# ScalarE copies a batch's turned probabilities ahead of the next batch's exponentials

## The reference

```python
xn, ln = layernorm(ctx), layernorm(layernorm(x))      # 64 + 64 rows a batch
q = ln @ Wq + bq
k, v = split(concat([xn, ln]) @ Wkv + bkv)
sim = einsum('bhid,bhjd->bhij', q * 128**-0.5, k)      # 8 heads x 64 x 128
out = einsum('bhij,bhjd->bhid', softmax(sim), v)
x = x + tanh(g_xattn) * (merge_heads(out) @ Wo + bo)
probs = softmax(layernorm(x) @ Wr + br); top 2 of 8 experts
x = x + tanh(g_ffn) * sum_e weight_e * (relu(layernorm(x) @ W1_e + b1_e) @ W2_e + b2_e)
```

## Time and profile before

| what | value |
|---|---|
| median of 3 runs | 795.09 us (794.71 to 797.86) |
| profiled execution: time | 800.09 us |
| profiled execution: span, first to last instruction | 798.4 us |
| granted TensorE clock, mean | 0.991 |
| busy: PE | 761.3 us, 95% of the span |
| busy: ACT | 497.8 us, 62% |
| busy: DVE | 525.9 us, 66% |
| busy: POOL | 443.1 us, 55% |
| DMA | 119.42 MB, mean 150 GB/s |

### The profile page before, as it was taken

The page is one execution under the profiler, slowest core; times in us unless marked ns, Lnnn a source line. Parts: engine busy times, 40 slices in busy tenths (PEclk is TensorE's granted clock), DMA queues, the critical chain, the costliest instruction groups (busy, mean ns, idle before and its releaser), DMA issues.

```text
span 798.4 us, 17460 instructions
## 1 busy us (share of the span) xinstructions
PE 761.3 (95%) x5392; PEld 645.5 (81%) x5392; DVE 525.9 (66%) x1829; ACT 497.8 (62%) x1630; POOL 443.1 (55%) x455
## 2 busy tenths in 40 slices
PE   7999999999999999999999999999999999879788
PEld 7778777777888988788988788988878889768665
DVE  4636677685857567677658777767768556465536
ACT  3677767676866566766556576656568655445622
POOL 2233264646552444785656686565668465466663
PEclk9999999999999999999999999999999999999999
DMA  6745151542455542174654146575316456534523
GB/s 196 199 161 193 59 210 71 210 145 81 145 186 158 200 153 71 41 231 160 214 195 146 47 109 219 189 230 172 104 44 199 146 191 205 162 107 122 149 77 87
DMA packets 119791, 119.42 MB, mean 150 GB/s; under 512 B 14585, under 2 KB 94994, under 8 KB 119698
## 3 DMA queue, kind: packets, MB, share of 16 engines
q1 hardware_dynamic: 111088, 102.41, 39.0%
q0 software_dynamic: 7680, 15.74, 6.7%
q10 hardware_dynamic: 930, 0.15, 0.1%
HBM read 35.94 MB, written 41.55 MB: 97 GB/s over the span
## 4 chain that ended last, share of the span: by engine, by line
PE 79%; DVE 6%; issue 6%; ACT 4%; POOL 2%; another core or an unknown queue 2%; DMA 1%; SPq 1%; ACTq 0%; DVEq 0%; POOLq 0%
PE shared L1426 14%; PE batch L1364 12%; PE batch L1377 12%; PE hid_ps L1294 8%; PE xy_ps L1308 7%; PE batch L1372 6%; PE shared L1217 3%; PE shared L1219 3%; PE shared L1218 3%; PE batch L1308 2%; ACT probs L746 2%; PE xy_ps L1271 2%; PE batch L1354 1%; PE shared L1415 1%
## 5 line engine op out<-in xcount | busy, mean ns | idle before, releaser
L676 POOL TENSOR_TENSOR probs<-probs,rsums 128x512 f32<-128x512 f32 x128 | 132.9, 1038 | 234.3 <-DVE rsums L1147 232.0
L746 ACT ACTIVATE probs<-batch,neg_max 128x128 f32<-128x128 f32 x512 | 180.5, 374 | 2.0 <-DVE neg_max L1151 2.0
L651 POOL DMA_INDIRECT sorted_x<-xn,row_of x120 | 121.3, 1011 | 36.0 <-issue 28.0
L827 ACT ACTIVATE qT<-shared,tb 128x512 f32<-128x512 f32 x128 | 87.2, 696 | 85.4 <-PE shared L1219 75.8
L1377 PE MATMUL batch<-pT_sb,kvn 128*128 128x512 f32 x256 | 134.2, 606 | 5.5 <-ACT pT_sb L754 5.4
L1364 PE MATMUL batch<-kvT,qT 128*128 128x128 f32 x1024 | 135.4, 275 | 0.8 <-ACT qT L827 0.8
L1426 PE MATMUL shared<-M,oT 128*128 128x128 f32 x1024 | 125.3, 275 | 0.2
L1364 PEld LDWEIGHTS batch<-kvT,qT 128*128 128x128 f32 x1024 | 124.4, 192 | 1.2 <-ACT qT L827 1.2
L1426 PEld LDWEIGHTS shared<-M,oT 128*128 128x128 f32 x1024 | 119.5, 192 | 1.3 <-issue 1.3
L746 ACT ACTIVATION_READ_ACCUMULATOR probs<-batch,neg_max 128x1 f32 x512 | 110.3, 215 | 0.0
L761 ACT ACTIVATE oT<-batch 128x512 f32<-128x512 f32 x128 | 76.2, 595 | 47.6 <-PE batch L1377 42.6
(11 more groups left out here) (168 smaller groups left out, 1241.7 us busy)
## 6 DMA issues: line engine op xcount, KB each, us to landing
wt<-wall SPq DMA_DIRECT2D x124, 321.0 KB
sorted_x<-yg SPq DMA_DIRECT2D x36, 512.0 KB, 4.9
xt<-sorted_x SPq DMA_DIRECT2D x162, 64.0 KB
sorted_y<-y_sb SPq DMA_DIRECT2D x78, 128.0 KB
kv<-in_ctx_dram SPq DMA_DIRECT2D x16, 256.0 KB
kv<-in_x_dram SPq DMA_DIRECT2D x16, 256.0 KB
xres<-in_x_dram SPq DMA_DIRECT2D x32, 128.0 KB
out_dram<-x SPq DMA_DIRECT2D x15, 256.0 KB
```

The lines of the kernel that those rows point to most:

```text
L651: nc.gpsimd.indirect_dma_start(xs[k % SETS][:, :], bass.IndirectOffsetOnAxis(ap=row_of[:, g, choice, c:c + 1], axis=0), xn[:, g % 2, c, :] ...
L676: nc.gpsimd.tensor_tensor(pv, pv, rsums[:, m % 2, :].unsqueeze(2).broadcast_to([P, 4, P]), ALU.mult).then_inc(probs_ready, 1)
L746: last = nc.scalar.activation(probs[:, m % 2, c * P:(c + 1) * P], batch_ps[m % BANKS][:, c * P:(c + 1) * P], ACT.Exp, bias=neg_max[:, m % ...
L827: nc.scalar.activation(qT[:, g % 2, :, number, :], sh[:, :].rearrange("p (b i) -> p b i", b=GB), ACT.Identity, bias=tb[:, number:number + ...
```

## The change

ACT's `slot(n)` copies the turned probabilities of batch n - 2 before the exponentials of batch n - 1. The operations, their waits and their numbers stay the same; only their order on ACT's list differs. The instructions of the other engines are the same.

```diff
             def slot(n):
                 if 0 <= n - OUT - 1 < B:
                     keep_product(n - OUT - 1)
+                if 0 <= n - TURN < B:
+                    keep_turned(n - TURN)
                 if 0 <= n - EXP < B:
                     exponentials(n - EXP)
-                if 0 <= n - TURN < B:
-                    keep_turned(n - TURN)
                 g = n // GB - 1
                 if n % GB == 6 and 0 <= g < G:
                     act.wait_ge(route_step, ROUTE * g + 2)
```

## The result

The changed kernel took 817.38 us (median of 4 runs, 816.08 to 819.68) against 796.47 us of the kernel before (median of 4, 794.71 to 797.86): a ratio of 1.0265, 95% interval 1.0241 to 1.0290, which is 19.2 to 23.1 us slower. The forecast was 817.0. The two totals agree better than the differences do: the forecast added 21.9 us to a median of 795.09, and the measured difference is 20.9 from a median that now stands 1.4 us higher. The profiled execution took 819.68 us, 19.59 more than that of before. Its page says where: PE is busy about as long as before (761.3 us there), in a span that is 19.6 us longer.

The account below looks back on a forecast made before the run. PE was taken to set the time throughout. Slots without tiles through POOL +10.7, queries behind DVE +11.2, tile slots and product 0: +21.9 us on the median 795.09 gives 817.0, range 803 to 829 (chance 0.80).

Parts of the forecast that it names:

- The ring: Turn, copy, exponentials, reciprocal, multiply, next turn: no slot beats 4.13 us; slots without tiles lose 10.7 us through POOL.
- The turn came as soon as it could.: Slot 40's turn followed POOL's multiply by 0.18 us, with no cover between a slot's exponentials and the next turn.
- The new wait, turn to copy: ACT's copy must now wait for PE's turn of the same slot, beginning 0.63 us after the turn's start.
- The other 18 waits: Turn waits for POOL outside places 7 and 1 without tiles: 0 to 0.57 us each, 0.15 taken, 2.7 us.
- The product's gain: PE's product stops waiting for ACT's copy: bounded by 13.7 us of loads or 5.4 us of idleness, taken as zero.
- Queries behind DVE: PE's queries wait longer for DVE's bank readings: logits 3.4, table 4.3, projection behind the homes 3.5, together 11.2 us.
- What would show it: Signs listed beforehand; among them, query loads wait 0.5 (logits), 1.1 (table) and 0.9 us (projection) longer each.
- Tile slots: In slots with tiles the multiply comes 1.32 us later against a cover of 4.31 us, costing 0.
- The copy was the bound: Rival, chance 0.05: PE's product stops waiting for ACT and the exponentials' delay is covered; 781.4 us at best, or 789.7.
- Nothing measurable: Rival, chance 0.07: the delays fall where PE has work anyway; 795 us, between 791 and 799.
- the tile slots pay too: Rival, chance 0.08: the 1.32 us shift reaches PE in tile slots; 857 us if in 30, 830 in ten.

Follow-up runs that it names:

- The experiment on the 15 slots alone: Copy ahead of the exponentials only in 15 slots without tiles with queries behind DVE (logits, table, projection), against the kernel before: 811.13 us, ratio 1.0172.
- the odd places: Kernel before with ACT's exponentials ahead of the product's copy at odd places only, even places unchanged: 790.56 us, ratio 0.9922.
- the experiment on them: Copy of the turned probabilities ahead of the exponentials in slots with a tile alone, against the kernel before: 799.78 us, ratio 1.0034.
- two moves on DVE: Kernel before with DVE's table copy ahead of its reciprocal and its search for home experts behind the projection's reading: 792.32 us, ratio 0.9947.

## Why the prediction was right, step by step

- *The ring.* The mechanism held: slots of 3.6 and 3.7 us became slots of 4.05 to 4.08, and with the five links of slot 39 as above slots 2, 7 and 39 take 4.07. Mis-sized was the last link, multiply to next turn: 1.21 forecast, 1.09 measured. Together with the turn-to-copy link, 0.69 instead of 0.63, the ring is 4.07, not 4.13. At place 7 without tiles the closeness is luck: the prediction had the copy wait for the turn there, and it is ACT's own copy of the product that sets the first link.
- *"The turn came as soon as it could."* That step was not quite so, and it is why 1.21 was too long. Rows of the kernel before that the prediction did not use, end of slot 39:

```profile
203.16 0.30 PEld L1377 LDWEIGHTS batch<-pT_sb,kvn 128*128 128x128 f32 x2 [0.29 <-ACT pT_sb L754]
203.17 1.12 PE L1377 MATMUL batch<-pT_sb,kvn 128*128 128x512 f32 x2
...
204.01 0.27 PEld L1372 LDWEIGHTS batch<-ident,probs 128*128 128x128 f32 x2 [0.55 <-POOL probs L676]
```

  The product was loaded 0.05 us after the copy ended (202.49 + 0.62 = 203.11), and PE went on from it to the turn at 204.13 without a gap, although the turn's load had waited 0.55 us for POOL. So copy and product set that turn; the multiply, done at 203.95, had 0.18 us, of which a turn that really waits for it needs 0.05 (211.45 - 211.40). There was a cover of 0.13 us. The delay of 0.49 less this cover is 0.36; place 7 lost 0.37 a slot.
- *The new wait, turn to copy.* ACT idled before the copy in 73 of slots 2 to 127, most, as forecast (in the kernel before, the turn ended such a wait in one, slot 12); 63 of the 73 copies begin within 0.06 us of the turn's end. The list names the turn for fewer, 52, because it gives "issue" for 20, that of slot 83 among them. But the place was partly wrong. At place 7 without tiles not one of 8 copies waited for the turn; the product's copy ahead of it sets the 0.69. At places 0 and 2 to 4 without tiles most copies did wait (0.39 us in slot 40). The wait shows its price in the table's slots: 1.21 us instead of the 0.49 of ACT's own work.
- *The other 18 waits.* 2.7 forecast, 3.41 measured, differently spread: slot 2 alone lost 1.55 (2.53 to 4.07 us), slots 3, 19 and 27 some 0.4 each, place 0 0.08 on average, while slots 5 and 6 became 0.31 and 0.22 shorter. No run tries these slots by themselves.
- *The product's gain.* Zero forecast, and little was there to have: of PE's own 5.4 us before the product 2.6 lie in slot 129, behind the last whole slot, and 1.1 in slot 5. The rest are waits of about 0.2 us, all but one in slots with a query behind the logits.
- *Queries behind DVE.* 11.2 forecast, 11.11 measured; in slots 37, 83 and 60 0.50, 1.21 and 0.88 against 0.49, at least 1.07 and 0.88. Slots 35 and 36 fall short of that: behind the table only 0.81, behind the homes 0.51. The experiment on the 15 slots alone gives 11.01. In "What would show it" I had given these amounts for the loads' own waits: those behind the logits grew by (13.9 - 6.9) / 7 = 1.0 us each, twice the slot's 0.50, because PE also reaches the query earlier, its product no longer waiting for the copy (2.92 us after the turn against 3.31). What the change gives to the product is lost at the next query.
- *Tile slots.* 0 forecast, 0.70 measured. Tile slots that lengthen were one of the prediction's signs of being wrong, and by this little they did; the multiply's cover in slot 76 shrank from 4.49 to 3.12 us (420.05 - 415.89 - 1.04) and held. DVE's outputs are not all read a slot later: the logits at place 5 are read in the same slot.
- *The rivals.* "The copy was the bound" describes a real 0.13 us per slot at place 7, and the 13.7 us of waiting went away, but the time rose: its deciding condition, 0.49 us to spare for the multiply, was not met. The rule of "Perfetto Trace Analysis" (Optimization Strategy) in the Trainium skill, to make the awaited dependency start sooner, is borne out here only where what is displaced has cover, as at the odd places (-6.3 us); with this change the loads' gap before L1377 closed, the one before L1372 grew from 17.4 to 37.3 us. "Nothing measurable" falls with the interval, "the tile slots pay too" with the experiment on them.

## What to carry to other kernels

To move an instruction earlier on an engine that takes its list in order is to move everything it jumps over later, by its length or by its wait, whichever ends last: before such a move, list every reader of the jumped work (here the next turn through DVE and POOL, and three kinds of queries through DVE) and subtract each one's own cover in the same slot. A wait of an engine's loads is not yet idle time of that engine: look at whether its matmuls were still busy at the time, as they were before the turn of slot 40 in the kernel before. What to reorder is found per kind of slot: the same move gained at odd places (-6.3 us) and lost at even ones, and two moves on DVE, off the bottleneck, gave another 3.7 us.

## What the runs showed that I had not expected

Executions of different kernels mostly repeat a slot's length to about 0.02 us where nothing that concerns it was changed (slots 67, 91 and 98 are exceptions in some executions, by 0.13 to 0.43 us), yet they reach slot 2 at times that differ: 34.89 us in the kernel before, 34.77 with the new order in tile slots, 33.23 with DVE's two moves, which touch nothing ahead of slot 35, and 32.42 after. Outside slots 2 to 127 the ten profiled executions spent 143.2 to 148.3 us, the most of them the kernel before. A difference of about 2 us between two spans can therefore stem from the start alone, and terms as small as these are read from slot lengths, not from the span.
